# The norm and the turns of a first FFN: norm by pairs of tiles, three tiles normalised on ScalarE, all turns copied by ScalarE out of four banks, and loads in another order

## The reference, cut to what matters

```python
x = x + 0.5 * ffn(_layernorm(x))
x = x + attn(_layernorm(x))
x = x + 0.5 * ffn(_layernorm(x))

def _layernorm(x, eps=1e-05):
    m = jnp.mean(x, axis=-1, keepdims=True)
    v = jnp.var(x, axis=-1, keepdims=True)
    return (x - m) / jnp.sqrt(v + eps)

# ffn(xt): 16 experts in 4 groups, the 2 best groups, then the 2 best experts of a row
logits = xt @ router_w + router_b
scores = softmax(logits) + router_bias
h = silu(xt @ w1 + b1) * (xt @ w2 + b2)          # per chosen expert, then gate * (h @ w3 + b3)
z = silu(xt @ sw1 + sb1) * (xt @ sw2 + sb2) @ sw3 + sb3   # shared expert, every row
```

## Time and profile before

| | us |
|---|---|
| median of 3 runs | 444.49 |
| lowest and highest | 444.15, 445.17 |
| the profiled execution | 446.19 |
| its span, first to last instruction | 444.1 |
| PE busy | 396.2 (89% of the span) |
| DVE busy | 258.7 (58%) |
| ACT busy | 177.2 (40%) |
| POOL busy | 176.4 (40%) |

### The profile page before, as it was taken

One profiled execution on the slowest core, in us unless ns is written; L12 is line 12 of the kernel. 1 busy time (PEld: TensorE's weight loads), 2 busy tenths in 40 slices (PEclk: granted clock), 3 DMA queues, 4 the chain that ended last, 5 costly groups with the idle time before them and its releaser, 6 DMA issues.

```text
span 444.1 us, 8313 instructions
## 1 busy us (share of the span) xinstructions
PE 396.2 (89%) x2788; PEld 278.8 (63%) x2789; DVE 258.7 (58%) x638; ACT 177.2 (40%) x302; POOL 176.4 (40%) x268
## 2 busy tenths in 40 slices
PE   0899899999969999989989989699999879999972
PEld 0677578888646767655555555244687568888660
DVE  4579633233367976787866775447449923333357
ACT  1321245666202322176654554544350336565300
POOL 2431325665302762455552463532001055666300
PEclk9999999999998999999999999979999989999997
DMA  7999994434397567223230110000420043534278
GB/s 233 291 376 315 316 330 154 167 113 142 120 320 262 146 153 201 75 88 98 60 117 27 59 51 13 24 32 18 155 96 1 0 143 117 161 121 154 86 282 332
DMA packets 51148, 66.05 MB, mean 149 GB/s; under 512 B 8286, under 2 KB 30470, under 8 KB 51076
## 3 DMA queue, kind: packets, MB, share of 16 engines
q1 hardware_dynamic: 42748, 43.55, 30.4%
q0 software_dynamic: 6368, 19.32, 13.9%
q10 hardware_dynamic: 2000, 2.76, 2.1%
HBM read 46.32 MB, written 19.79 MB: 149 GB/s over the span
## 4 chain that ended last, share of the span: by engine, by line
PE 63%; DVE 15%; DMA 11%; issue 4%; SPq 3%; ACT 1%; POOL 1%; ACTq 0%; POOLq 0%; DVEq 0%
PE ps L1589 15%; PE ps L1596 7%; PE ps L1658 7%; PE ps L1738 6%; PE ps L1453 5%; PE ps L1574 4%; PE ps L1714 3%; PE ps L1686 3%; DMA turns<-in_L_ffn_sw_dram 3%; DMA arena<-xn_dram,arena 2%; PE ps L1688 2%; SPq L394 2%; PE ps L1700 2%; PE ps L1666 2%; DVE arena L1265 2%
## 5 line engine op out<-in xcount | busy, mean ns | idle before, releaser
L1265 DVE TENSOR_REDUCE arena<-ps 128x3 f32<-128x384 f32 x128 | 69.5, 554 | 34.4 <-PE ps L1688 32.3
L1589 PE MATMUL ps<-arena,wj 128*128 128x128 f32 x608 | 74.9, 276 | 0.0
L1589 PEld LDWEIGHTS ps<-arena,wj 128*128 128x128 f32 x608 | 72.0, 194 | 1.0 <-issue 1.0
L862 ACT ACTIVATE arena<-ps 128x768 f32<-128x768 f32 x64 | 51.2, 810 | 45.1 <-PE ps L1702 44.2
L648 POOL TENSOR_SCALAR_AFFINE_SELECT arena<-arena 128x512 f32<-128x512 f32 x64 | 40.6, 639 | 58.8 <-ACT arena L862 58.2
L1160 DVE SCALAR_TENSOR_TENSOR arena<-ps,arena 128x128 f32<-128x128 f32 x38 | 13.3, 350 | 81.6 <-ACT arena L754 81.6
L1453 PE MATMUL ps<-arena,turns 128*128 128x256 f32 x256 | 57.6, 381 | 0.7 <-DMA turns<-in_L_ffn_sw_dram 0.7
L1453 PEld LDWEIGHTS ps<-arena,turns 128*128 128x128 f32 x256 | 48.1, 190 | 9.1 <-issue 2.1
L554 POOL DMA_INDIRECT arena<-xn_dram,arena x34 | 33.2, 977 | 51.0 <-DVE arena L1100 25.2
L559 POOL DMA_INDIRECT y_dram<-arena x38 | 38.4, 1011 | 34.9 <-DVE arena L1167 26.0
L1596 PE MATMUL ps<-w,arena 128*128 x76 | 39.1, 596 | 0.6 <-DVE arena L1160 0.6
(11 more groups left out here) (196 smaller groups left out, 589.7 us busy)
## 6 DMA issues: line engine op xcount, KB each, us to landing
arena<-y_dram SPq DMA_DIRECT2D x16, 512.0 KB, 7.6
arena<-q_dram SPq DMA_DIRECT2D x48, 128.0 KB, 2.7
xn_dram<-arena SPq DMA_DIRECT2D x16, 256.0 KB, 6.0
w<-in_L_ffn_ew_dram SPq DMA_DIRECT2D x4, 1024.0 KB, 11.0
q_dram<-arena SPq DMA_DIRECT2D x16, 192.0 KB, 2.5
x<-_attn_hidden_states_dram SPq DMA_DIRECT2D x4, 512.0 KB, 6.4
out_dram<-x SPq DMA_DIRECT2D x8, 256.0 KB, 5.6
arena<-arena SPq DMA_DIRECT2D x30, 64.0 KB
```

Of the source, the lines that this page charges most:

```text
L862: act.activation(pr[:, n % 2, pair, :], ps[:, bank:bank + 2, :].rearrange("p a b -> p (a b)")[:, 0:768], ACT.Exp).then_inc(sem("exp"), 1)
L1265: dve.tensor_reduce(m3[:, h // (HEADS // 2), :, h % (HEADS // 2)], ps[:, bank, 0:3 * P].rearrange("p (n k) -> p n k", n=3), AX_X, ALU.max) ...
L1589: ins = pe.matmul(o, wj[:, par, c, n * INTER:(n + 1) * INTER], xgT[:, par, c, :], start=(c == 0), stop=(c == KC - 1))
```

## The change

- The norm goes by pairs: `LN` now has four pairs for both ffns, and DVE does sums and statistics of one pair after the other. POOL computes four rstd of two tiles each.
- ScalarE normalises tiles 2, 3 and 7 (`ACT_ROWS`) as `Identity(scale * x + bias)`, with rstd as scale and -mean * rstd as bias. DVE makes that bias (`ln_shift`, written over `varE`) for the second and the fourth pair. PE and SP wait for those tiles on their own semaphore (`xn_wait`).
- ScalarE copies all eight turns. They use four banks in place of two, so turn t waits for copy t - 4.
- Loads: `cb` is issued by POOL behind the last rstd; the shared weights are issued by ACT after `x_in1`; SP waits for `x_in3` before `shb` and all that stands behind it.

```diff
--- before.py
+++ after.py
@@ -40,7 +40,7 @@
 LEAD = 5
 LAST = LEAD
 BIASED = 3
-DVE_TURNED = (5, 7)
+ACT_ROWS = (2, 3, 7)
 LN_AT = (None, None, 4, 3)
 EARLY = 2
 JP = 32
@@ -292,7 +292,7 @@
         block = ctx.enter_context(nc.Block())
 
 
-        LN = ((range(0, NT // 2), range(NT // 2, NT)), tuple(range(QT * b, QT * (b + 1)) for b in range(BATCH)))
+        LN = tuple(range(QT * b, QT * (b + 1)) for b in range(BATCH))
 
 
         ITEMS = (0, 1, None, 2, 3)
@@ -326,10 +326,18 @@
 
             eng.dma_start(kT[0:R_REST, b], k_dram[b].rearrange("d r t -> (d r) t")).then_inc(sem(f"q_in{b % 2}0"), 16)
 
+        def xn_wait(eng, f, t):
+
+            of_act = sum(n <= t for n in ACT_ROWS)
+            if f == 0 and t in ACT_ROWS:
+                eng.wait_ge(sem("xn_act"), of_act)
+            else:
+                eng.wait_ge(sem("xn"), t + 1 - of_act if f == 0 else NT - len(ACT_ROWS) + t + 1)
+
         def ffn_sp(f):
             for t in range(NT):
 
-                nc.sync.wait_ge(sem("xn"), NT * f + t + 1)
+                xn_wait(nc.sync, f, t)
                 nc.sync.dma_start(xn_dram[t * P:(t + 1) * P, :], xn[:, t, :]).then_inc(sem("xn_out"), 16)
             if f == 1:
 
@@ -472,6 +480,7 @@
             sp.dma_start(rw[:, :, 0:E], rw_in.rearrange("(c p) e -> p c e", p=P)).then_inc(sem("small_in"), 16)
             sp.dma_start(rbc[:, 0, :], rb_in.partition_broadcast(P)).then_inc(sem("small_in"), 16)
             sp.dma_start(rbc[:, 1, :], rbias_in.partition_broadcast(P)).then_inc(sem("small_in"), 16)
+            sp.wait_ge(sem("x_in3"), 16)
             sp.dma_start(shb[:, 0, :], sb1.rearrange("(c p) -> p c", p=P), allow_slow_non_contiguous=True).then_inc(sem("shb_in"), 16)
             sp.dma_start(shb[:, 1, :], sb2.rearrange("(c p) -> p c", p=P), allow_slow_non_contiguous=True).then_inc(sem("shb_in"), 16)
             for n in range(len(EPART)):
@@ -530,15 +539,16 @@
             link(pool.tensor_tensor(part(5)[:, :, 0, :], grest[:], part(3)[:, :, 0, :], ALU.subtract))
 
         def ln_rstd(f, n):
-            nc.gpsimd.wait_ge(sem("var"), 2 * f + n + 1)
-            at = slice(LN[f][n][0], LN[f][n][-1] + 1)
+            nc.gpsimd.wait_ge(sem("var"), BATCH * f + n + 1)
+            at = slice(LN[n][0], LN[n][-1] + 1)
             nc.gpsimd.tensor_tensor(rstd[:, at], varE[:, at], neghalf[:, at], ALU.pow).then_inc(sem("rstd"), 1)
 
         def ffn_pool(f):
             pool = nc.gpsimd
             if f == 0:
-                ln_rstd(0, 0)
-                ln_rstd(0, 1)
+                for n in range(BATCH):
+                    ln_rstd(0, n)
+                pool.dma_start(cb[:], const_b).then_inc(sem("cb_in"), 16)
                 bias_parts()
             gate_parts(f)
             pool.wait_ge(sem("jex"), f + 1)
@@ -678,7 +688,6 @@
         @block.gpsimd
         def _(pool):
             pool.memset(rw[:], 0.0).then_inc(sem("pool_set"), 1)
-            pool.dma_start(cb[:], const_b).then_inc(sem("cb_in"), 16)
             pool.memset(neghalf[:], -0.5).then_inc(sem("pool_set"), 1)
             for g in range(1, E // EG):
                 pool.memset(mark[:, g:g + 1], 0.0).then_inc(sem(f"ew_in{g}"), 1)
@@ -690,12 +699,10 @@
 
 
         def xn_bank(f, t):
-            return (PS_XT if f == 0 else PS_S) + t % 2
+            return (PS_XT, PS_XT + 1, PS_Y, PS_Y + 1)[t % 4] if f == 0 else PS_S + t % 2
 
         def xnT_copy(f, t):
             nc.scalar.wait_ge(sem("xt"), NT * f + t + 1)
-            if f == 0 and t > DVE_TURNED[0]:
-                nc.scalar.wait_ge(sem("xnT"), t)
             nc.scalar.copy(xnT[:, t].rearrange("p c q -> p (c q)"), ps[:, xn_bank(f, t), :]).then_inc(sem("xnT"), 1)
 
         def ffn_act(f):
@@ -709,9 +716,11 @@
 
             if f == 1:
                 shared_silu(0)
-            for t in range(NT) if f == 0 else LN[1][-1]:
-                if f == 1 or t not in DVE_TURNED:
-                    xnT_copy(f, t)
+            for t in range(NT) if f == 0 else LN[-1]:
+                if f == 0 and t in ACT_ROWS:
+                    act.wait_ge(sem("shift"), 1 if t < NT // 2 else 2)
+                    act.activation(xn[:, t, :], x[:, t, :], ACT.Identity, bias=varE[:, t:t + 1], scale=rstd[:, t:t + 1]).then_inc(sem("xn_act"), 1)
+                xnT_copy(f, t)
             if f == 1:
                 shared_silu(1)
             act.wait_ge(sem("lt"), f + 1)
@@ -896,7 +905,7 @@
             act.dma_start(cf[:], const_f).then_inc(sem("cf_in"), 16)
             act.wait_ge(sem("pool_set"), 2)
             act.copy(mark[:, 0:1], neghalf[:, 0:1])
-            act.wait_ge(sem("x_in2"), 16)
+            act.wait_ge(sem("x_in1"), 16)
             act.dma_start(sw12[:, :, 0:SHARED], sw1.rearrange("(c p) f -> p c f", p=P)).then_inc(sem("sw_in"), 16)
             act.dma_start(sw12[:, :, SHARED:], sw2.rearrange("(c p) f -> p c f", p=P)).then_inc(sem("sw_in"), 16)
             act.dma_start(sw3s[:], sw3.rearrange("(c p) d -> p c d", p=P)).then_inc(sem("sw_in"), 16)
@@ -907,34 +916,40 @@
 
 
 
-        def ln_sums(tiles):
+        def ln_sums(n):
 
             dve = nc.vector
-            dve.wait_ge(sem(f"x_in{tiles[0] // 2}"), 16)
-            for t in tiles:
+            dve.wait_ge(sem(f"x_in{n}"), 16)
+            for t in LN[n]:
                 ins = dve.bn_stats(st[:, t, :], x[:, t, :])
-            if tiles[-1] in (LN[0][0][-1], LN[0][1][-1]):
-                ins.then_inc(sem("ln"), 1)
+            ins.then_inc(sem("ln"), 1)
 
         def ln_stats(f, n):
 
             dve = nc.vector
-            tiles = LN[f][n]
             if f == 0:
-                dve.wait_ge(sem("ln"), 2 * n + 1)
+                dve.wait_ge(sem("ln"), n + 1)
             else:
-                dve.wait_ge(sem("stats"), tiles[-1] + 1)
-            for t in tiles:
+                dve.wait_ge(sem("stats"), LN[n][-1] + 1)
+            for t in LN[n]:
                 ins = dve.bn_aggr(mv[:, t, :], st[:, t, :])
-            ins.then_inc(sem("ln"), 1)
-            dve.wait_ge(sem("ln"), 2 * n + 2 if f == 0 else 5 + n)
-            at = slice(tiles[0], tiles[-1] + 1)
+            ins.then_inc(sem("aggr"), 1)
+            dve.wait_ge(sem("aggr"), BATCH * f + n + 1)
+            at = slice(LN[n][0], LN[n][-1] + 1)
             dve.tensor_scalar(varE[:, at], mv[:, at, 1], EPS, None, ALU.add).then_inc(sem("var"), 1)
 
+        def ln_shift(n):
+
+            dve = nc.vector
+            at = slice(LN[n][0], LN[n][-1] + 1)
+            dve.wait_ge(sem("rstd"), n + 1)
+            dve.scalar_tensor_tensor(out=varE[:, at], in0=mv[:, at, 0], scalar=-1.0, in1=rstd[:, at],
+                                     op0=ALU.mult, op1=ALU.mult).then_inc(sem("shift"), 1)
+
         def ln_rows(f, t):
 
             dve = nc.vector
-            dve.wait_ge(sem("rstd"), 2 * f + 1 + [t in tiles for tiles in LN[f]].index(True))
+            dve.wait_ge(sem("rstd"), BATCH * f + t // QT + 1)
             dve.tensor_scalar(xn[:, t, :], x[:, t, :], mv[:, t, 0:1], rstd[:, t:t + 1],
                               ALU.subtract, ALU.mult).then_inc(sem("xn"), 1)
 
@@ -962,23 +977,24 @@
                                          op0=ALU.add, op1=ALU.mult).then_inc(sem("s_h"), 1)
 
             if f == 0:
-                ln_sums((0, 1))
-                ln_sums((2, 3))
+                ln_sums(0)
                 ln_stats(0, 0)
-                ln_sums((4, 5))
+                ln_sums(1)
+                ln_stats(0, 1)
                 ln_rows(0, 0)
                 ln_rows(0, 1)
-                ln_sums((6, 7))
-                ln_stats(0, 1)
-                for t in range(2, NT):
-                    ln_rows(0, t)
-                for t in DVE_TURNED:
-                    dve.wait_ge(sem("xt"), t + 1)
-                    dve.wait_ge(sem("xnT"), t)
-                    dve.tensor_copy(xnT[:, t].rearrange("p c q -> p (c q)"), ps[:, xn_bank(0, t), :]).then_inc(sem("xnT"), 1)
+                ln_shift(1)
+                ln_sums(2)
+                ln_stats(0, 2)
+                ln_sums(3)
+                ln_stats(0, 3)
+                ln_rows(0, 4)
+                ln_rows(0, 5)
+                ln_shift(3)
+                ln_rows(0, 6)
             else:
                 ln_stats(1, BATCH - 1)
-                for t in LN[1][-1]:
+                for t in LN[-1]:
                     ln_rows(1, t)
                 shared_h(0)
                 shared_h(1)
@@ -1434,8 +1450,10 @@
 
         def xn_turn(f, t):
             pe = nc.tensor
-            pe.wait_ge(sem("xn"), NT * f + t + 1)
-            if t >= 2:
+            xn_wait(pe, f, t)
+            if f == 0 and t >= 4:
+                pe.wait_ge(sem("xnT"), t - 3)
+            elif f == 1 and t >= 2:
                 pe.wait_ge(sem("xnT"), NT * f + t - 1)
             for c in range(KC):
                 ins = pe.transpose(ps[:, xn_bank(f, t), c * P:(c + 1) * P], xn[:, t, c * P:(c + 1) * P], ident)
```

## The result

The change made the kernel slower, and by twice what I forecast: 449.66 us median of 11 runs (445.77 to 451.56) against 444.69 (443.76 to 446.59) in 11 runs of before. The ratio is 1.0101, 95% interval 1.0073 to 1.0128. I forecast +2.5 us and got +5.0 by the medians (+4.5 by the ratio, interval +3.2 to +5.7); my range ended at 448.8. The direction and the place were right, the size was not. All ratios here leave out runs over 1.5% above the fastest of the same kernel, and the medians don't, so the two can differ a little.

A forecast was written before the change was run, and what follows sets the result against it. The prediction took PE's start on the shared matmuls, ended by the shared weights' load, as the bound. Router +2.05, slack -0.73 and low clock +1.2 gave +2.5 us on the 444.49 median: 447.0 us, 8 in 10 range 444.2 to 448.8.

The forecast's parts named there:

- Norm by pairs: Start of the first ffn: with statistics per pair, rows 0 and 1 start at 8.75, not 10.43, 1.7 us gained.
- ScalarE's row: Normalising one 128x512 tile on ScalarE: 0.65 us taken, between 0.59 and 0.69.
- The ladder: Tiles 2, 3 and 7: row, turn and copy go in sequence, 2.45 us each; router +1.6 to +2.05 us.
- Slack and loads: Before the shared matmuls: 0.73 us slack subtracted; weights land by 20.0, masks at 22.5, later small loads are covered.
- The low clock, in the router: Router and logits' transposes at 1.2 GHz: +1.8 us if all low; two thirds taken, +1.2.
- The low clock, behind the router: First shared matmuls at low clock: at most 1.5 us more, counted only in the upper end, 449.1.
- The sum: Whole kernel: router +2.05, slack -0.73, low clock +1.2, giving +2.5 us on the median, 447.0 us.
- late router, clock high: Rival: same late router, but the clock rises and stays; +0.7 to +1.3 us, 445.2 to 445.8; chance 0.22.

The follow-up runs named there:

- hoist: Changed kernel with ScalarE's rows 2 and 3 written ahead of copy 0 and row 7 ahead of copy 3; 446.61 us, ratio 1.0040.
- dve_rows: Changed kernel with ScalarE's three rows back on DVE, everything else kept; 446.13 us, ratio 1.0017.
- before_again: The unchanged kernel executed once more for a second profile; 443.05 us.
- old_loads: Changed kernel with the loads in their old order (masks first, shared weights after x_in2, small loads at once); 450.43 us, ratio 1.0150.
- after_late: Changed kernel with x loaded only after an added memset on DVE, to start all work later; 449.81 us, ratio 1.0081.
- after_again: The changed kernel run again unaltered, for its spread and a second profile; 451.09 us, ratio 1.0126.
- warm: Changed kernel with PE's gaps filled by unread transposes, 22 before the first turn, then 8, 8, 8 and 4; 446.36 us, ratio 1.0022.
- warm_cb: As warm, with the masks (cb) issued first again; 447.22 us, ratio 1.0058.
- hoist_cb: As hoist, with the masks (cb) issued first again; 446.55 us, ratio 1.0045.
- hoist_cb_warm: As hoist_cb, plus unread PE transposes, 22 before the first turn, then 2, 3 and 4; 446.16 us, ratio 1.0023.
- hoist_cb_fill: As hoist_cb, plus unread PE transposes around the list in the first ffn (10, 5 and 4); 445.58 us, ratio 1.0048.

## Where the prediction held and where it failed

- **Norm by pairs.** Right. Rows 0 and 1 at 8.56 (I said 8.75), first turn at 9.25 (9.4), rstd of two tiles 0.72 and 0.92 us (I took 1.04).
- **ScalarE's row.** I took 0.65 between 0.59 and 0.69. It is 0.72 in the chain, above my upper bound: the 128x256 operations of the earlier trace rows, out of PSUM and with a bias alone, did not bound one out of SBUF with a scale as well. The 0.10 that the earlier trace rows give for a bias pointer, taken once more for the scale pointer, would have made 0.79, an estimate near the 0.81 shown for a single one; no run separates the two pointers.
- **The ladder.** Right in place, order and size: 2.50 us a rung (2.45), router at 21.2 to 21.7 in four profiles (21.4 to 21.9). hoist and dve_rows remove it and the router stands at 18.0 and 17.5.
- **Slack and loads.** The weights no longer end the wait, as I said, but the slack of 0.73 us was that of one execution: before_again has none, and the term is then 0. The masks land at 22.4 (22.5), by luck, since they were issued 1.2 us earlier than I took and flew 8.3 us in place of 7.1; they cost nothing behind a late router. POOL did wait for the small loads, 7.73 us until 22.70, and nobody behind it did.
- **The low clock, in the router.** "I take two thirds, +1.2" came out in the profiles: the router takes 2.97 to 3.54 us against 2.02, on the mean 1.19 more, and the transposes of the logits 0.15 more. All low it takes 3.67 (old_loads, after_late), where I had priced 3.5.
- **The low clock, behind the router.** This is the step that failed: the term ended with the logits, and the sum said that "the shift holds in any execution". It does not. In after_late and old_loads the clock stays low into the shared matmuls, and the first job is 4.1 and 4.4 us late. In after_again it falls once more in the first job, and the +1.9 become +4.2. I had low shared matmuls as the upper end of the forecast's own range (449.1), and cut it off in the range that I gave; low clock in the jobs I had at nothing.
- **The sum.** The forecast was +2.5. The first job comes at 59.98 to 60.26 in the four profiles of after and at 58.07 and 57.18 in the two of before: on the means +2.5. That the number is met so closely is luck, since it mixes a slack of 0.73 and one of 0. The runs have +5.0, so half of the loss is not in the sum. The rival "late router, clock high", +0.7 to +1.3, is what warm measures: +1.0 us (0.9990 to 1.0054), though there the shorter turns brought the router forward as well.

Where the rest of the +5.0 is stays open; two readings fit in part. By the profiles it is low clock behind the first job: the four of after (449.2 to 453.6 us, all above my range) have the +2.5 and 22 to 30 us of low clock behind the router, against 20 and 14. But the mean granted clock of all 11 runs of after, 0.978, is no lower than that of before (0.979 to 0.981 in the series), so this does not carry over to most of them.

The other reading is a clock that rises as late as in after_late. The granted clock's column reads 1.00 until its first record, whatever the durations say, so such a rise leaves no mark in a run's mean clock. The run's time less the recorded low part (444 times one less the clock) is 435.3 to 436.1 on the mean over the runs of before and 436.8 in the first profiled execution of after; but it is 439.6 on the mean over after's 11 runs, and up to 442.7, 440.8 in old_loads and 439.6 in after_late. So some timed executions of after may go that way. It is not shown: all four profiles of after went the first way, and warm and warm_cb, whose clock is up from 10.4 and 7.2 in their profiles, give 438.5 and 438.3 by the same sum. Between 2 and 3 us of such a rest come without a late rise.

Two more things stay open. The variants with an early list (warm_cb, hoist_cb, hoist_cb_warm, hoist_cb_fill) are 1.0 to 2.6 us slower than before by their ratios, with the list up to 1.9 us ahead of its first profile's and 1.0 us ahead of its second's. A fall explains part of it in hoist_cb (at the first job) and in hoist_cb_warm (at 47.8, where 16 matmuls take 5.38 us in place of 3.70), and none of it in warm_cb and hoist_cb_fill. And I did not find what decides where the falls behind 130 us land, each of which costs up to half its length.

## What to carry to other kernels

On an engine that works in order, write all that can be ready early ahead of what waits for another engine: rows written between the copies put round trips of 2.5 us into turns that had overlapped. Before moving work out of a stretch in which TensorE runs without a gap, ask whether that stretch is what brings its clock up, and ask of every stage behind it, not only of the next one, what it costs at the low clock. Take a slack from more than one profile: the 0.73 us here was one late load. And compare medians of many runs: a stage 2 us earlier in one profile was worth nothing here.

## What the runs showed of the hardware

- Short waits can cost the clock too: in after it fell at 22.0 behind gaps of 1.39 and 0.67 us, and the router took 3.25 us in place of 2.02. The same ladder with filled gaps kept the clock. Not all such waits do: warm keeps its clock through 0.99 and 0.52 us at the first job, hoist_cb loses it behind 1.18 and 0.54.
- The granted clock's column is no witness before its first record: it reads 1.00 while four transposes take 1.11 us, and 0.66 once it is really high.
- An ACTIVATE of 128x512 from SBUF, scale and bias by pointer, is shown with 0.81 us (0.72 in the chain); the copy of that shape out of PSUM has 0.59.
- The same program moved by 3 us between two profiled executions: 0.8 from when one load lands, most of the rest with where TensorE's clock falls (one fall at 134.0 more, 1.5 us; mean clock 0.978 and 0.985).
